# A scan-and-feed-forward kernel on one core: the last tile's chain in two halves of time, eight parked partial sums that GpSimd adds in, earlier biases, and a second queue for the last stores

## The reference, cut to what matters

```python
tf    = sigmoid(sum(cond));  decay = exp(-exp(w)) * (0.5 + 0.5 * tf)
ek    = exp(min(k, 30));     ekv = ek * k
nf,df = forward scans over time of ekv, ek with decay;  nb,db = backward scans
euk   = exp(min(u + k, 30))
num   = nf + nb - ekv + euk * k;   den = df + db - ek + euk
y     = sigmoid(x) * num / max(den, 1e-8) * (0.8 + 0.2 * tf)
out   = x + y @ (sign(W) * mean|W|).T + bias
```

## Time and profile before

| | us |
|---|---|
| median of 3 runs | 534.18 (533.85 to 538.0) |
| the profiled execution | 535.11 |
| its span (first to last record) | 533.4 |
| busy, share of the span: VectorE / TensorE / ScalarE / GpSimd | 93% / 69% / 73% / 68% |
| end of the last denominator (start of the tail) | 482.5 |
| last result written by VectorE | 527.4 |

### The profile page before, as it was taken

How to read it: one execution, slowest core, us unless ns; L and a number is a source line. 1 busy time by engine, 2 the same in 40 slices (tenths; PEclk the granted TensorE clock), 3 DMA queues, 4 the chain that set the end, 5 groups by cost and what they waited for, 6 DMA issues and landing times.

```text
span 533.4 us, 5364 instructions
## 1 busy us (share of the span) xinstructions
PE 365.5 (69%) x1797; PEld 212.1 (40%) x1803; DVE 498.4 (93%) x379; ACT 388.8 (73%) x424; POOL 363.9 (68%) x194
## 2 busy tenths in 40 slices
PE   2333323333678886787777997975499999796994
PEld 1222212222334443444444554543345555442441
DVE  4999999999999999999999999999999999996692
ACT  2869889797859999999969797987776776744000
POOL 0057666767667887777978778877967778878300
PEclk9999999999998798797899897987789999798998
DMA  6754576665664899988887888998766887768998
GB/s 187 208 139 137 157 174 166 165 168 121 153 157 105 176 194 197 187 163 161 167 180 177 190 175 181 197 197 188 156 130 166 190 183 173 159 118 158 203 220 327
DMA packets 125923, 92.65 MB, mean 174 GB/s; under 512 B 2860, under 2 KB 117576, under 8 KB 125896
## 3 DMA queue, kind: packets, MB, share of 16 engines
q0 software_dynamic: 30720, 33.56, 39.9%
q1 hardware_dynamic: 93096, 57.70, 36.7%
q10 hardware_dynamic: 2080, 1.05, 0.7%
HBM read 58.74 MB, written 16.78 MB: 142 GB/s over the span
## 4 chain that ended last, share of the span: by engine, by line
DVE 66%; issue 20%; PE 9%; ACT 2%; POOL 1%; DMA 1%; DVEq 0%; SPq 0%; ACTq 0%; POOLq 0%
DVE pair L722 25%; DVE pair L736 14%; DVE pair L748 7%; DVE wkv L765 7%; DVE own L749 6%; DVE pair L745 4%; PE sT L425 3%; DVE euk L770 2%; PE kT L425 1%; PE prod L425 1%; PE prod L389 1%; DVE y_start L728 1%; PE cols L425 1%; PE yT L425 1%; ACT rec L576 1%
## 5 line engine op out<-in xcount | busy, mean ns | idle before, releaser
L389 PE MATMUL prod<-acts,sgn 128*128 128x512 f16 x768 | 192.7, 408 | 6.1 <-ACT orow L659 3.1
L736 DVE TENSOR_TENSOR_SCAN pair<-cols,y_start,pair 128x1024 f32<-128x1024 f32 x64 | 150.1, 2347 | 1.3 <-DVE y_start L728 0.2
L722 DVE TENSOR_TENSOR_SCAN pair<-cols,pair 128x1024 f32<-128x1024 f32 x64 | 142.8, 2272 | 0.0
L389 PEld LDWEIGHTS prod<-acts,sgn 128*128 128x128 f16 (+1 forms) x768 | 80.3, 105 | 100.2 <-issue 24.3
L336 POOL TENSOR_TENSOR wkv<-wkv,rec 128x1024 f32<-128x1024 f32 x31 | 73.3, 2364 | 42.5 <-ACT wkv L614 42.5
L364 PE MATMUL kT<-ident,k_nat 128*128 128x128 f32 x256 | 47.6, 348 | 77.6 <-DVE own L749 77.6
L329 POOL TENSOR_TENSOR wkv<-euk,rec 128x1024 f32<-128x1024 f32 x31 | 77.9, 2514 | 32.4 <-ACT rec L578 32.4
L343 POOL TENSOR_TENSOR wkv<-wkv,pair 128x1024 f32<-128x1024 f32 x31 | 73.2, 2360 | 11.9 <-DVE wkv L765 11.7
L576 ACT ACTIVATE rec<-euk,lnb 128x1024 f32<-128x1024 f32 x32 | 36.7, 1148 | 53.9 <-DVE euk L770 53.8
L299 POOL TENSOR_TENSOR acts<-wkv,rec 128x1024 f16<-128x1024 f32 x31 | 73.9, 2383 | 2.0 <-ACT rec L587 2.0
L364 PEld LDWEIGHTS kT<-ident,k_nat 128*128 128x128 f32 x256 | 38.8, 181 | 84.1 <-issue 84.1
(11 more groups left out here) (99 smaller groups left out, 518.7 us busy)
## 6 DMA issues: line engine op xcount, KB each, us to landing
pair<-own POOLq DMA_DIRECT2D x32, 512.0 KB, 4.6
k_nat<-in_fside_BxSxS_dram SPq DMA_DIRECT2D x30, 512.0 KB, 3.8
x_nat<-in_x_dram SPq DMA_DIRECT2D x29, 512.0 KB, 5.8
o_nat<-in_x_dram POOLq DMA_DIRECT2D x24, 512.0 KB, 6.2
out_dram<-o_nat SPq DMA_DIRECT2D x24, 512.0 KB, 5.4
x_end<-in_x_dram SPq DMA_DIRECT2D x9, 512.0 KB, 6.1
y_fm<-in_L_ffn_weight_dram SPq DMA_DIRECT2D x8, 512.0 KB, 6.3
x_nat<-in_L_ffn_bias_dram POOLq DMA_DIRECT2D x3, 512.0 KB, 9.3
```

Of the source, the lines that this page charges most:

```text
L389: ins = pe.matmul(prod[:, h, :], view[:, c, m % CT * P:m % CT * P + P], acts[:, part, m // CT % 2 * CT + c, h * H:(h + 1) * H], start=(par ...
L722: dve.tensor_tensor_scan(buf, d, buf, 0.0, ALU.mult, ALU.add).then_inc(st["F" + kind], 1)
L736: dve.tensor_tensor_scan(buf[:, ::-1], d, buf[:, ::-1], y_start[:, i:i + 1], ALU.mult, ALU.add)\
```

## The change

- **Last tile by halves.** The last tile's denominator, reciprocal, refinement, gate, product and split are done for time steps 512 to 1023 first (i = 0), then for 0 to 511 (i = 1), on VectorE and ScalarE. The low half of tile 30 moves from GpSimd to VectorE (`prior_lo`). `rows_of` turns the order of the last batch's rows so that v = 0 to 7 lie in the half that is ready first. The second `last_lo` stands behind the first result (v = 0) on VectorE.
- **Eight partial sums.** v = 8 to 15 all have their first four channel tiles made in steps 30 and 31 (`begun`), and ScalarE parks them (`park`). After `last_lo` 2, GpSimd scales each parked sum and adds it to x (two operations of 128x512 for each), and VectorE waits for that (`joined`) before its own last add.
- **Biases.** Six of the eight bias DMAs go into GpSimd's steps 26 to 31, behind chk; the last two and the last three residuals wait for `last_lo` 2.
- **Order in steps 26 to 31.** `s_turn` comes first on TensorE. `low_half(n-2)` comes after `base(n-1)` in GpSimd's steps 26 to 29. The last tile's numerator DMA goes ahead of `base(30)`.
- **Stores.** The last three `o_nat` tiles are stored from ScalarE's queue.

```diff
-early_part = [y_fm[0][:, 0:H], y_fm[0][:, H:T], y_fm[1][:, 0:H]]
+park = [acts[:, 0, i, :].bitcast(F32) for i in range(CT)]
...
-bank = [prod[:, 0, :], prod[:, 1, :], kT[:, 0:H], kT[:, H:T],
-        yT[:, :, :].rearrange("p q f -> p (q f)"), cols[:, :], sT[:, 0:H], sT[:, H:T]]
+yT_flat = yT[:, :, :].rearrange("p q f -> p (q f)")
+bank = [kT[:, 0:H], kT[:, H:T], prod[:, 0, :], yT_flat, prod[:, 1, :], cols[:, :], sT[:, H:T], sT[:, 0:H]]
+park_bank = [prod[:, 0, :], prod[:, 1, :], prod[:, 0, :], yT_flat, prod[:, 1, :], prod[:, 0, :], yT_flat,
+             prod[:, 1, :]]
+def time_half(i):
+    return slice(H, T) if i == 0 else slice(0, H)
...
+def rows_of(j):
+    q = (j + TT // 2) % TT
+    return slice(q * P, (q + 1) * P)
+def natural(a, j):
+    return a[B - 1, rows_of(j), :]
...
     run(step)
-    for n in range(N, added[-1] + 1):
-        stores(n)
...
+        if n >= N - TT + 2:
+            biases(n - N + TT - 2)
...
+        late = N - 6 <= n < N - 2
         if low and first:
...
         if mid:
...
-        if low and not first:
+        if low and not first and not late:
...
+        if n == N - 1:
+            done(pool, "yn", n)
+            pool.dma_start(ekv[p], own[p][:, :], accum_op=ALU.add).then_inc(num_in[p], 16)
         if mid:
...
+        if late:
+            low_half(n - 2, p)
...
     run(step)
...
-    done(pool, "yn", N - 1)
-    pool.dma_start(ekv[1], own[1][:, :], accum_op=ALU.add).then_inc(num_in[1], 16)
-    for q in range(3):
-        biases(q)
-    low_half(N - 2, 0)
-    for q in range(3, TT):
-        biases(q)
+    pool.wait_ge(st["last_lo"], 2)
...
+    for j in range(TT - 2, TT):
+        biases(j)
+    pool.wait_ge(st["orow_sb"], 1)
+    for i in range(CT):
+        j, h = TT // 2 + i // 2, i % 2
+        o = slice(h * H, (h + 1) * H)
+        pool.wait_ge(st["early_sb"], i + 1)
+        pool.tensor_tensor(park[i], park[i], orow[:, o], ALU.mult).then_inc(st["weighed"], 1)
+        pool.wait_ge(st["weighed"], i + 1)
+        pool.wait_ge(b_in[j], 16)
+        pool.tensor_tensor(x_tail(j)[:, o], x_tail(j)[:, o], park[i], ALU.add).then_inc(st["joined"], 1)
...
 @block.tensor
 def _(pe):
...
+    def begun(i):
+        done(pe, "lo", N - 6)
+        across(TT + i, park_bank[i], range(CT - 5), True, False)
+        done(pe, "lo", N - 5)
+        across(TT + i, park_bank[i], range(CT - 5, CT - 4), False, True).then_inc(st["early"], 1)
     def across(v, dst, tiles, begin, end):
...
     def step(n, p, wt, nxt, nxt3, mid, low, out):
+        if n >= N - 2:
+            s_turn(n - 1)
+        if n == N - 2:
+            done(pe, "ev", 2 * LAST - 2)
+            begun(0)
+            k_turn(n + 1, 1 - p)
+            turned(2 * LAST - 1)
+            begun(1)
+            pe.wait_ge(st["early_sb"], 1)
+            begun(2)
+            done(pe, "yc", 2 * LAST - 1)
+            begun(3)
+            pe.wait_ge(st["early_sb"], 2)
+            begun(4)
+            pe.wait_ge(st["early_sb"], 3)
+            begun(5)
+        if n == N - 1:
+            pe.wait_ge(st["early_sb"], 4)
+            begun(6)
+            pe.wait_ge(st["early_sb"], 5)
+            begun(7)
+        if n >= N - 2:
+            return
...
+        sooner = N - 6 <= n
+        if sooner:
+            s_turn(n - 1)
...
-        if n == N - 1:
-            done(pe, "lo", N - 4)
-            for v in (0, 1):
-                across(v, bank[v], range(CT - 4, CT - 3), False, False)
-        if mid:
+        if mid and not sooner:
...
-        if n == N - 2:
-            done(pe, "ev", 2 * LAST - 2)
-            done(pe, "lo", N - 5)
-            across(0, bank[0], range(CT - 4), True, False)
-            turned(2 * LAST - 1)
-            across(8, bank[1], range(CT - 4), True, True).then_inc(st["early"], 1)
-            done(pe, "yc", 2 * LAST - 1)
-            across(9, bank[4], range(CT - 4), True, True).then_inc(st["early"], 1)
-            pe.wait_ge(st["early_sb"], 1)
-            across(1, bank[1], range(CT - 4), True, False)
-            pe.wait_ge(st["early_sb"], 2)
-            across(10, bank[4], range(CT - 4), True, True).then_inc(st["early"], 1)
...
     run(step)
...
-    for v in (2, 3):
+    done(pe, "lo", N - 4)
+    for v in (0, 1):
...
-    pe.wait_ge(st["early_sb"], 3)
+    pe.wait_ge(st["early_sb"], 6)
+    across(2, bank[2], range(CT - 3), True, False)
+    pe.wait_ge(st["early_sb"], 7)
+    across(3, bank[3], range(CT - 3), True, False)
+    s_turn(N - 1)
+    pe.wait_ge(st["early_sb"], 8)
...
     for v in range(5):
...
-    s_turn(N - 1)
...
-    done(pe, "gate", N - 1)
-    done(pe, "lo", N - 2)
-    for v in (6, 7):
-        across(v, bank[v], range(CT - 1), True, False)
+    pe.wait_ge(st["last_gate"], 1)
+    across(6, bank[6], range(CT - 2), True, False)
+    def ended(v, lo):
+        across(v, bank[v % TT], range(lo, CT), v >= TT, True).then_inc(st["nat"], 1)
+    pe.wait_ge(st["prior_lo"], 1)
...
-    for v in range(2 * TT):
-        if v >= 8:
-            done(pe, "res", v - 8)
-        tiles = range(CT - 2 if v < 6 else CT - 1 if v < 8 else CT - 4 if v < 11 else 0, CT)
-        across(v, bank[v % 8], tiles, v >= 8, True).then_inc(st["nat"], 1)
+    for v in range(3):
+        ended(v, CT - 2)
+    pe.wait_ge(st["last_gate"], 2)
+    across(7, bank[7], range(CT - 2), True, False)
+    for v in range(3, TT):
+        ended(v, CT - 2)
+    pe.wait_ge(st["prior_lo"], 2)
+    pe.wait_ge(st["last_lo"], 2)
+    for v in range(TT, 2 * TT):
+        done(pe, "res", v - TT)
+        ended(v, CT - 4)
...
 @block.scalar
 def _(act):
...
     def early_out(i):
...
-        act.copy(early_part[i], bank[1 if i == 0 else 4]).then_inc(st["early_sb"], 1)
+        act.copy(park[i], park_bank[i]).then_inc(st["early_sb"], 1)
...
     def step(n, p, wt, nxt, nxt3, mid, low, out):
         if mid:
...
+        if n == N - 2:
+            clear(cleared(n - 1), cleared(n))
+        if n == N - 1:
+            early_out(4)
+            early_out(5)
         if low:
...
-        if out:
+        if out and n < N - 2:
...
-        if n == N - 1:
-            early_out(2)
         if mid:
...
         if n == N - 2:
+            early_out(0)
...
-        if n > LAST + 1:
+        if n == N - 1:
+            early_out(6)
+            early_out(7)
+        if LAST + 1 < n < N - 2:
...
         if n == N - 2:
-            early_out(0)
-            early_out(1)
+            for i in (1, 2, 3):
+                early_out(i)
...
-            clear(sooner, later)
+            if n < N - 2:
+                clear(sooner, later)
...
-        if out:
+        if out and n < N - 2:
...
     run(step)
...
-    inverse(N - 1, 1)
+    def last_inverse(i):
+        t = time_half(i)
+        act.wait_ge(st["last_den"], i + 1)
+        act.activation(rec[1][:, t], euk[1][:, t], ACT.Ln, bias=lnb[:, 0:1]).then_inc(st["last_ln"], 1)
+        act.wait_ge(st["last_ln"], i + 1)
+        act.activation(rec[1][:, t], rec[1][:, t], ACT.Exp, scale=-1.0).then_inc(st["last_rec"], 1)
+    def last_halves(i):
+        t = time_half(i)
+        high = acts[:, 0, (N - 1) % (2 * CT), t]
+        act.wait_ge(st["last_base"], i + 1)
+        act.mul(high, wkv[1][:, t], 1.0 / LO_GAIN).then_inc(st["last_hi"], 1)
+        act.wait_ge(st["last_hi"], i + 1)
+        act.mul(rec[1][:, t], high, LO_GAIN).then_inc(st["last_hib"], 1)
+    done(act, "lo", N - 3)
+    last_inverse(0)
...
-    act.wait_ge(st["last_base"], 1)
-    halves(N - 1, 1)
+    last_inverse(1)
+    last_halves(0)
+    last_halves(1)
+    for n in range(N, added[-1] + 1):
+        for m in summed(n):
+            act.wait_ge(res_in[m % NO], m // NO * 16 + 16)
+            act.dma_start(tile_of(out, m), o_nat[m % NO][:, :, :]).then_inc(o_out[m % NO], 16)
...
 @block.vector
 def _(dve):
...
-        dve.scalar_tensor_tensor(U, U, E30, E, ALU.min, ALU.add).then_inc(st["den"], 1)
+        if n < N - 1:
+            dve.scalar_tensor_tensor(U, U, E30, E, ALU.min, ALU.add).then_inc(st["den"], 1)
...
     run(step)
...
-    W, R, S = wkv[1][:, :], rec[1][:, :], HI_SCALE * LO_GAIN
-    done(dve, "rec", N - 1)
-    dve.scalar_tensor_tensor(W, euk[1][:, :], -S, R, ALU.mult, ALU.mult).then_inc(st["last_chk"], 1)
-    dve.wait_ge(st["last_chk"], 1)
-    dve.scalar_tensor_tensor(W, W, 2.0 * S, R, ALU.add, ALU.mult).then_inc(st["last_inv"], 1)
-    dve.wait_ge(st["last_inv"], 1)
-    done(dve, "sT", N - 1)
-    dve.scalar_tensor_tensor(W, W, S / DEN_MIN, sT[:, :], ALU.min, ALU.mult).then_inc(st["gate"], 1)
-    done(dve, "gate", N - 1)
-    landed(dve, num_in, N - 1, 1)
-    dve.tensor_tensor(W, W, ekv[1], ALU.mult).then_inc(st["last_base"], 1)
-    done(dve, "hib", N - 1)
-    dve.tensor_tensor(acts[:, 1, (N - 1) % (2 * CT), :], W, R, ALU.subtract).then_inc(st["last_lo"], 1)
+    S = HI_SCALE * LO_GAIN
+    def last_den(i):
+        t = time_half(i)
+        dve.scalar_tensor_tensor(euk[1][:, t], euk[1][:, t], E30, ek[1][:, t], ALU.min, ALU.add)\
+           .then_inc(st["last_den"], 1)
```

(68 more changed lines are left out.)

## The result

The changed kernel takes 540.55 us (540.41 to 542.2, 4 runs) against 534.97 of the kernel before, measured beside it (534.46 over 16 later runs). The ratio is 1.0102 with a 95% interval of [1.0054, 1.015]: slower by about 1%, above the 539.5 that the prediction had named for that, and outside its range of 525.5 to 536.3. The profiled execution took 542.2, 1.7 above the median, with a span of 540.1.

A forecast was written before the change was run, and what follows sets the result against it. VectorE was taken to bound the loop, TensorE's matmuls the 51 us tail. With the loop 2.75 us later and GpSimd ending the shortened tail, the span goes from 533.4 to 529.9: median 530.6, range 525.5 to 536.3.

The forecast's parts named there:

- Part 1, the moved low halves: Loop, steps 26 to 29: GpSimd's low half behind the base product delays Ln; the loop ends 2.75 us later.
- the period of 15.87: Loop, gates of steps 27 to 30: forecast spacing in us between gates behind moved low halves, where it was 14.7.
- The shift: How much later the loop ends: forecast 2.75 us, with bounds of 1.3 earlier and 7.3 later.
- the rival in which den loses: GpSimd's low half gets in before VectorE's den, steps 26 to 29: 2.3 us a step, shift 7.3; chance 0.13.
- 0.58 and 0.95 won less four times 0.13: Loop's low-cost bound: early s_turn and avoided den stall won, 0.13 us lost a step; stated as 1.3 earlier.
- a shift of 6.3: Loop delay in us from which the change was said to turn slower, given as 1.9 us a step.
- Part 2, the early biases: GpSimd, steps 26 to 31: bias issues of about 1 us each fit idle time of 1.63 and cost nothing.
- Part 3, TensorE: TensorE up to the first sum: 26.3 us from den(30)'s end, ready at 494.1 plus the loop's delay.
- 2.84 of Ln, Exp and copy: Wait after den(30) ahead of the last two begun sums: Ln and Exp 2.24 us, copy 0.6.
- Part 4, what ends last: Tail after the first sum: GpSimd ends last, 522.75 plus the loop's delay, 5 us behind TensorE and VectorE.
- GpSimd: 3 residual issues and 2 biases: Tail, GpSimd: five DMA issues priced at 6.5 us, ahead of 16 operations in pairs of 2.5.
- The last stores: End of span: SyncE's last store lands in 3.2 us, 0.4 to the end; ScalarE's three stores cost nothing.

The follow-up runs named there:

- the PSUM clamp: Changed kernel, low half still late, clamps of steps 27 to 30 written with their second input in PSUM: 538.81 us, ratio 1.0075.
- the run with the early DMAs: Changed kernel with low half ahead of the base product and the last two bias, then three residual DMAs right behind base(30): 519.97 us, ratio 0.971.

## Why the prediction was wrong

- **Part 1, the moved low halves.** The step that failed is the list of what the low half can meet. Den holding it (to 3.35, forecast 3.3), Ln's wait and the period of 15.87 (measured 16.0 with the PSUM clamp) were right. But of VectorE's operations only den was considered, as one with two SBUF inputs. The clamp, which starts as den ends, has one such input, and is held 2.1 us each time. Its price was the hint: 0.74 for 1024 columns, where VectorE's other operations of that width take 1.2 or, as the scans, more. The Trainium skill (SBUF — State Buffer, "SBUF: two separate sides") names both kinds, an operation "in a 2-port perf mode, or with two SBUF inputs"; the prediction used the second half alone. The rows agree with the whole sentence (0.74 alone, 2.85 beside the low half, 1.21 and not held with a PSUM input). The shift was 6.4, not 2.75: +3.7 on the forecast. That comes near the 7.3 of the rival in which den loses, but by another mechanism: den took 1.23 and not 3.5. Two figures at the edges don't follow from their terms: 0.58 and 0.95 won less four times 0.13 is 1.0 earlier, not 1.3, and a shift of 6.3 needs 2.1 us a step by the reckoning that gives 7.3, not 1.9. Neither touches the forecast.
- **Part 2, the early biases.** Right: nothing. In the run with the early DMAs six biases are issued inside the loop, and from the gate near 387 to the last gate it takes 90.23, as in the kernel before (387.52 to 477.75).
- **Part 3, TensorE.** The matmuls are priced right, one wait is not: from den(30)'s end (474.18) to the first sum it took 24.6 in place of 26.3. The forecast has 2.84 of Ln, Exp and copy ahead of the last two begun sums. TensorE started the first of the two at 474.34 and then waited 0.75.
- **Part 4, what ends last.** GpSimd did end last, with `last_lo` 2 to the first product's end as forecast (8.1 against 7.7) and pairs of 2.57 (forecast 2.5). The step that failed is "GpSimd: 3 residual issues and 2 biases": it priced the issue of the last two biases and never asked when they land. They cost 8.65 us of stall. The signs were in the kernel before: the issues of three residuals took 6.40 in the tail, and the view of landings, which the rows ahead don't show, has a longest one of 16.2 for the biases (L305) and of 23.6 for the residuals (L312):

```profile
DMA to landing us min/median/max: 7.3/10.8/16.2
DMA to landing us min/median/max: 6.0/6.2/23.6
```

- **The last stores.** Forecast 3.6 from the last add to the end, measured 2.5: -1.1.

The sum: 3.7 - 1.7 + 8.65 + 0.7 (pairs and first product) - 1.1 = 10.2, from a span of 529.9 to 540.1. With one of the two mistakes undone the kernel takes 535.29 or 537.39, with both 532.27, 1.7 above the forecast. There the last add ends at 524.0, ahead of the forecast 526.3, and what is left are the residuals' stores, which the prediction had called free.

## What to carry to other kernels

Before an operation of GpSimd is moved, list every VectorE operation that its new interval can touch, those with two SBUF inputs and those with one that run faster than the usual price for their width; each of them may stand still until GpSimd is through. Price a DMA by its landing, not by its issue, and look at what is ahead of it in its queue and how small those packets are. An engine's idle time before a wait is room for issuing, though not always for computing: here moving five DMAs in front of the wait, biases first, turned 540.55 into 526.91, and the low halves back in their place made it 519.97, 3% below the kernel before.

## What the runs showed of the hardware

- A clamp with one f32 input and output in SBUF (0.74 us for 128x1024) was held by GpSimd's subtraction to 2.85 and ended 0.55 after it; written with its second input in PSUM it took 1.21 and was not held.
- Where VectorE's and GpSimd's operations of 128x512 with two SBUF inputs ran side by side, both took 1.7, in place of 0.68 and 1.27.
- Two bias DMAs of 512 KB landed in 25 us (median) behind three DMAs of together 3072 packets of 512 bytes, in 14.3 behind the same three issued 18 us earlier, and in 6.6 to 7.3 ahead of the three (9.1 where GpSimd's products ran beside them).
- A store of 256 KB landed in 2.0 us in the changed kernel, in 4.6 to 4.8 where the residuals' stores ran until the end, and in 5.2 in the kernel before.
- A granted clock of 0.71 to 0.75 in place of 1.00 during 5 us (395 to 400) went with a loop that ended some 1.65 later, in two different kernels.
